# Four-token attention: relative scores by TensorE from folded weights, four of eight projections in front of the norm's last transposes, softmax in two halves

## The reference

```python
qkv = jnp.einsum('tbe,fe->tbf', query, in_proj_weight) + in_proj_bias
q, k, v = jnp.split(qkv, 3, axis=-1)
q = q * scaling                      # 8 ** -0.5
q, k, v = (heads(q), heads(k), heads(v))       # (b*16, t, 8)
dist = jnp.clip(r[None, :] - r[:, None], -L, L) + L
rel_k = rel_pos_keys[dist][:, :, :D]
scores = jnp.einsum('btd,bsd->bts', q, k) + jnp.einsum('btd,tsd->bts', q, rel_k)
probs = jax.nn.softmax(scores, axis=-1)
attn = jnp.einsum('bts,bsd->btd', probs, v)
return jnp.einsum('tbe,oe->tbo', attn, out_w) + out_b
...
x = _layernorm(x + _L2_attn_ref(x, ...), axis=-1)
```

## Time and profile before

| | before |
|---|---|
| median of three runs | 1515.82 us (1515.19 to 1516.74) |
| the profiled execution | 1518.54 us |
| its span | 1516.8 us |
| PE, DVE, ACT, POOL busy | 86%, 61%, 45%, 26% |
| mean granted clock of TensorE | 0.95 of 2.4 GHz |
| chain that ended last | PE 68%, DVE 18%, ACT 6%, issue 4%, POOL 4% |

### The profile page before, as it was taken

The page is one execution under the profiler, slowest core; times in us unless marked ns, Lnnn a source line. Parts: engine busy times, 40 slices in busy tenths (PEclk is TensorE's granted clock), DMA queues, the critical chain, the costliest instruction groups (busy, mean ns, idle before and its releaser), DMA issues.

```text
span 1516.8 us, 23793 instructions
## 1 busy us (share of the span) xinstructions
PE 1308.2 (86%) x8985; PEld 834.7 (55%) x8985; DVE 928.5 (61%) x2179; ACT 676.6 (45%) x1915; POOL 398.8 (26%) x326
## 2 busy tenths in 40 slices
PE   7999986888787878868987379899898999999997
PEld 4666663565555533325564345556565666666664
DVE  2555577666664689986755777555674555653343
ACT  4555444465664465524642035523345555432322
POOL 1333104443432177736100252010001333400000
PEclk9999999999999998979998699999999999999999
DMA  9000000000000054410002200000000000000000
GB/s 392 20 1 1 1 1 1 1 1 1 1 1 2 26 149 124 123 48 1 2 1 112 112 1 2 1 1 1 1 3 1 1 1 1 1 1 1 0 7 8
DMA packets 13280, 43.75 MB, mean 29 GB/s; under 512 B 1776, under 2 KB 3952, under 8 KB 12528
## 3 DMA queue, kind: packets, MB, share of 16 engines
q1 hardware_dynamic: 13168, 42.24, 8.2%
HBM read 41.58 MB, written 0.66 MB: 28 GB/s over the span
## 4 chain that ended last, share of the span: by engine, by line
PE 68%; DVE 18%; ACT 6%; issue 4%; POOL 4%; DMA 1%; DVEq 0%; SPq 0%; POOLq 0%; ACTq 0%
PE PS L1147 6%; PE PS L692 6%; PE PS L1097 4%; PE PS L1098 4%; PE PS L335 4%; DVE PS L2237 4%; PE PS L367 4%; PE PS L347 3%; PE PS L758 3%; PE PS L308 2%; PE PS L316 2%; PE PS L376 2%; PE PS L329 2%; PE PS L310 2%; DVE arena L2244 2%
## 5 line engine op out<-in xcount | busy, mean ns | idle before, releaser
L559 POOL TENSOR_TENSOR arena<-arena,small 128x768 f32<-128x768 f32 (+1 forms) x64 | 107.8, 1684 | 226.6 <-DVE small L502 117.7
L916 DVE TENSOR_REDUCE arena<-PS 128x2 f32<-128x512 f32 (+1 forms) x192 | 108.8, 609 | 54.9 <-PE PS L686 53.9
L850 ACT ACTIVATE arena<-PS 128x512 f32<-128x512 f32 (+1 forms) x192 | 92.2, 532 | 106.4 <-PE PS L692 106.4
L1243 DVE TENSOR_TENSOR arena<-arena,PS 128x512 f32<-128x512 f32 x82 | 56.3, 687 | 109.9 <-ACT arena L1107 109.8
L1107 ACT ACTIVATE arena<-PS 128x512 f32<-128x512 f32 x82 | 49.0, 598 | 162.0 <-PE PS L1098 162.0
L2044 PE MATMUL PS<-arena,w_consts 128*128 128x512 f32 x128 | 86.1, 761 | 34.1 <-DVE arena L2244 32.0
L439 ACT ACTIVATE arena<-PS,small 128x256 f32<-128x256 f32 (+1 forms) x256 | 110.8, 453 | 0.0
L692 PE MATMUL PS<-arena 32*128 32x256 f32 (+1 forms) x768 | 96.8, 368 | 14.0 <-DVE arena L916 9.0
L686 PE MATMUL PS<-arena 32*128 32x256 f32 (+1 forms) x768 | 93.8, 369 | 2.3 <-DVE arena L916 1.6
L510 DVE COPY arena<-PS 128x768 f32<-128x768 f32 (+1 forms) x64 | 69.5, 1086 | 34.5 <-PE PS L347 34.5
L2288 POOL TENSOR_TENSOR arena<-arena 128x512 f32<-128x512 f32 x64 | 80.4, 1270 | 36.4 <-DVE PS L2237 27.1
(11 more groups left out here) (408 smaller groups left out, 3021.4 us busy)
## 6 DMA issues: line engine op xcount, KB each, us to landing
arena<-rows SPq DMA_DIRECT2D x32, 512.0 KB, 4.8
w_last<-in_last SPq DMA_DIRECT2D x1, 8260.0 KB, 22.3
w_rest<-in_rest SPq DMA_DIRECT2D x1, 6463.5 KB, 38.1
w_last<-in_first SPq DMA_DIRECT2D x1, 4917.5 KB, 22.1
w_last<-in_first SPq DMA_DIRECT2D x1, 2176.0 KB, 10.2
w_last<-in_mid SPq DMA_DIRECT2D x1, 768.0 KB, 4.2
X<-in_x SPq DMA_DIRECT2D x1, 512.0 KB, 4.3
CT<-in_ctxT SPq DMA_DIRECT2D x1, 512.0 KB, 10.9
```

What stands on the lines that cost most here:

```text
L559: g.tensor_tensor(p, p, ri, ALU.mult).then_inc(self.pn_done.sem, 1)
L850: a.activation(self.PT[:, q % 8, :], PS[:, 3 + q % 3, 0:2 * n], ACT.Exp).then_inc(self.e_done.sem, 1)
L916: v.tensor_reduce(dst, src, AX.X, ALU.max, negate=True).then_inc(self.mx_done.sem, 1)
```

## The change

The relative part of the scores is linear in x: q times the relative keys is x times (query weights times relative keys), plus the query bias times the relative keys. One matmul folds the weights (`wqt` with `rel`, a block matrix of the relative keys by head), ScalarE copies the product into `fold`, and eight matmuls of 64 columns a tile give all relative scores in bank 6, on top of a matmul that writes the bias part. VectorE multiplies queries and keys straight from QKV and adds bank 6 afterwards; POOL has nothing to do. The scale moves into Exp. L2a becomes the norm's lead: the fold and projections 0 to 3 stand in front of the transposes of tiles 6 and 7, in place of five warming passes; the four warming passes behind the transposes are gone. Maxima, subtraction, Exp, sums, reciprocal and normalisation work on tiles 0 to 3 and 4 to 7 apart, the first half's maxima while products are still to come. Values times probabilities is one instruction a tile, not four; the subtraction and the normalisation one a half. Seven warming passes wait for the second subtraction. The output bias is written into banks 6 and 7 by a matmul with one row of ones, ahead of the output projection, which adds to it.

```diff
             self.transposes(pe, len(self.groups) - 1)
-            if not isinstance(self.lead, Experts):
+            if not isinstance(self.lead, (Experts, FourTokenAttention)):
                 keep_warm(self.c, pe, 3, 4)
...
+    def project(self, pe, n):
+        c = self.c
+        if n >= 4:
+            pe.wait_ge(self.p_ev.sem, self.p_ev.at(0, n - 3))
+        pe.matmul(c.PS[:, 2 + n % 4, 0:384], c.XT[:, n * P:(n + 1) * P], self.win, start=True, stop=True)\
+            .then_inc(self.p_done.sem, 1)
+    def lead_tensor(self, pe):
+        c = self.c
+        c.wait_weights(pe, self)
+        pe.matmul(c.PS[:, 7, 0:256], self.wqt, self.rel, start=True, stop=True).then_inc(self.fold_done.sem, 1)
+        pe.wait_ge(self.x_ready.sem, self.x_ready.at(0, 1 if self.led else 2))
+        for n in range(4):
+            self.project(pe, n)
+    def lead_scalar(self, a):
+        self.c.wait_weights(a, self)
+        a.wait_ge(self.fold_done.sem, self.fold_done.at(0, 1))
+        a.activation(self.fold, self.c.PS[:, 7, 0:256], ACT.Copy).then_inc(self.fold_ev.sem, 1)
     def tensor(self, pe):
         c, PS = self.c, self.c.PS
+        if not self.led:
+            self.lead_tensor(pe)
+        pe.matmul(PS[:, 6, :].rearrange("p (t u k) -> p t u k", t=4, u=2), self.bq.to_broadcast([P, P]),
+                  self.rel.rearrange("p (t k) -> p t k", t=4).unsqueeze(2).to_broadcast([P, 4, 2, 64]),
+                  start=True, stop=False, skip_group_check=True)
         pe.wait_ge(self.x_ready.sem, self.x_ready.at(0, 2))
+        for n in range(4, T):
+            self.project(pe, n)
+        pe.wait_ge(self.fold_ev.sem, self.fold_ev.at(0, 1))
         for n in range(T):
-            if n >= 4:
-                pe.wait_ge(self.p_ev.sem, self.p_ev.at(0, n - 3))
-            pe.matmul(PS[:, 2 + n % 4, 0:384], c.XT[:, n * P:(n + 1) * P], self.win, start=True, stop=True)\
-                .then_inc(self.p_done.sem, 1)
+            ins = pe.matmul(PS[:, 6, n * 64:n * 64 + 64], c.XT[:, n * P:(n + 1) * P],
+                            self.fold[:, n // 2 * 64:n // 2 * 64 + 64], start=False, stop=n == T - 1, skip_group_check=True)
+        ins.then_inc(self.rel_done.sem, 1)
+        pe.wait_ge(self.sh_ready.sem, self.sh_ready.at(0, 2))
+        keep_warm(c, pe, 7, 7)
         for n in range(T):
             pe.wait_ge(self.pv_ready.sem, self.pv_ready.at(0, n + 1))
-
             for k in range(4):
                 ins = pe.matmul(PS[:, n // 4, (n % 4) * P:(n % 4) * P + P], self.PV[:, n % 4, k * P:(k + 1) * P],
                                 c.ident, start=(k == 0), stop=(k == 3), skip_group_check=True)
-            if n < 3:
-                ins.then_inc(self.pv_used.sem, 1)
+            ins.then_inc(self.pv_used.sem, 1)
             if n % 4 == 3:
-                ins.then_inc(self.at_done.sem, 1)
+                pe.matmul(PS[:, 6 + n // 4, :].rearrange("p (t f) -> p t f", t=4), c.one[0:1, :].to_broadcast([1, P]),
+                          self.bout[0:1, :].unsqueeze(1).to_broadcast([1, 4, P]), start=True, stop=False,
+                          skip_group_check=True).then_inc(self.at_done.sem, 1)
         for n in range(T):
             if n % 4 == 0:
                 pe.wait_ge(self.at_ev.sem, self.at_ev.at(0, n // 4 + 1))
             ins = pe.matmul(PS[:, 6 + n // 4, (n % 4) * P:(n % 4) * P + P], self.AT[:, n * P:(n + 1) * P], self.wout,
-                            start=True, stop=True)
+                            start=False, stop=True, skip_group_check=True)
             if n % 4 == 3:
                 ins.then_inc(self.y_done.sem, 1)
     def scalar(self, a):
         c, PS = self.c, self.c.PS
-        a.wait_ge(self.sh_ready.sem, self.sh_ready.at(0, 1))
-        a.activation(self.sc, self.sc, ACT.Exp).then_inc(self.e_ready.sem, 1)
+        if not self.led:
+            self.lead_scalar(a)
+        for i in range(2):
+            a.wait_ge(self.sh_ready.sem, self.sh_ready.at(0, i + 1))
+            sc = self.sc[:, 4 * i:4 * i + 4, :]
+            a.activation(sc, sc, ACT.Exp, scale=8.0 ** -0.5).then_inc(self.e_ready.sem, 1)
         for i in range(2):
             a.wait_ge(self.at_done.sem, self.at_done.at(0, i + 1))
             a.activation(self.AT[:, i * 512:(i + 1) * 512], PS[:, i, :], ACT.Copy).then_inc(self.at_ev.sem, 1)
     def gpsimd(self, g):
...
+        pass
...
         v.wait_ge(self.p_ev.sem, self.p_ev.at(0, T))
...
+        def products(n):
+            pd = self.PD[:, n % 2, :]
+            v.tensor_tensor(pd.rearrange("p (s f) -> p s f", s=4), self.QKV[:, n % 2:T:2, 128:256],
+                            self.QKV[:, n, 0:128].unsqueeze(1).to_broadcast([P, 4, P]), ALU.mult).then_inc(self.prod.sem, 1)
+        def sums(n):
+            v.wait_ge(self.prod.sem, self.prod.at(0, n + 1))
+            return v.tensor_reduce(self.sc[:, n, :], self.PD[:, n % 2, :].rearrange("p (g d) -> p g d", d=8), AX.X, ALU.add)
+        def half(i):
+            r = slice(4 * i, 4 * i + 4)
+            sc, mx = self.sc[:, r, :], self.mx[:, r, :]
+            return (sc, mx, sc.rearrange("p n (s h) -> p n h s", s=4), sc.rearrange("p n (s h) -> p n s h", s=4),
+                    mx.unsqueeze(2).to_broadcast([P, 4, 4, 16]))
+        products(0)
         for n in range(T):
...
+            if n + 1 < T:
+                if n >= 1:
+                    link(sums(n - 1))
+                products(n + 1)
+            if n == T - 1:
+                sums(n - 1)
+                link(sums(n))
+            if n in (5, T - 1):
+                i = n // 6
+                sc, mx, by_head, by_key, spread = half(i)
+                if i == 0:
+                    v.wait_ge(self.rel_done.sem, self.rel_done.at(0, 1))
+                link(v.tensor_tensor(sc, sc, PS[:, 6, i * 256:i * 256 + 256].rearrange("p (n k) -> p n k", n=4), ALU.add))
+                link(v.tensor_reduce(mx, by_head, AX.X, ALU.max))
+                v.tensor_tensor(by_key, by_key, spread, ALU.subtract).then_inc(self.sh_ready.sem, 1)
+        for i in range(2):
+            sc, mx, by_head, by_key, spread = half(i)
+            v.wait_ge(self.e_ready.sem, self.e_ready.at(0, i + 1))
+            link(v.tensor_reduce(mx, by_head, AX.X, ALU.add))
+            link(v.reciprocal(mx, mx))
+            link(v.tensor_tensor(by_key, by_key, spread, ALU.mult))
+            for n in range(4 * i, 4 * i + 4):
+                if n >= 4:
                     v.wait_ge(self.pv_used.sem, self.pv_used.at(0, n - 3))
...
+                val = self.QKV[:, n % 2:T:2, 256:384].rearrange("p s (h d) -> p s h d", d=8)
+                p = by_key[:, n % 4].unsqueeze(3).to_broadcast([P, 4, 16, 8])
+                v.tensor_tensor(self.PV[:, n % 4, :].rearrange("p (s h d) -> p s h d", s=4, h=16), val, p, ALU.mult)\
+                    .then_inc(self.pv_ready.sem, 1)
         for i in range(2):
             v.wait_ge(self.y_done.sem, self.y_done.at(0, i + 1))
-            z = c.Z[:, 4 * i:4 * i + 4, :]
-            y = PS[:, 6 + i, :].rearrange("p (t f) -> p t f", t=4)
-            link(v.tensor_tensor(z, y, c.X[:, 4 * i:4 * i + 4, :], ALU.add))
-            ins = v.tensor_tensor(z, z, self.bout.unsqueeze(1).to_broadcast([P, 4, P]), ALU.add)
+            ins = v.tensor_tensor(c.Z[:, 4 * i:4 * i + 4, :], PS[:, 6 + i, :].rearrange("p (t f) -> p t f", t=4),
+                                  c.X[:, 4 * i:4 * i + 4, :], ALU.add)
         ins.then_inc(self.z_ready.sem, 1)
...
     rel = w["L2_attn_rel_pos_keys"][13:20, 0:8]
+    by_head = np.zeros((16, 8, 4, 4, 16), np.float32)
+    for h in range(16):
+        by_head[h, :, :, :, h] = np.stack([rel[3 - t:7 - t].T for t in range(4)], 1)
     l2a = [("L2a_win", w["L2_attn_in_proj_weight"].T), ("L2a_bin", over(w["L2_attn_in_proj_bias"])),
-           ("L2a_rel", np.broadcast_to(np.tile(rel, (1, 16)), (P, 7, P))), ("L2a_wout", w["L2_attn_out_w"].T),
+           ("L2a_wqt", w["L2_attn_in_proj_weight"][0:P]), ("L2a_bq", w["L2_attn_in_proj_bias"][0:P, None]),
+           ("L2a_rel", by_head.reshape(P, 256)), ("L2a_fold", np.zeros((P, 256), np.float32)), ("L2a_wout", w["L2_attn_out_w"].T),
            ("L2a_bout", over(w["L2_attn_out_b"]))]
...
-            if isinstance(s, (TwoWay, Experts)) or isinstance(s, NarrowAttention) and s.band is None:
+            if isinstance(s, (TwoWay, Experts, FourTokenAttention)) or isinstance(s, NarrowAttention) and s.band is None:
                 end.lead, s.led = s, True
```

More of the change, by code:

```diff
@@ L1799, with __init__ @@
 class FourTokenAttention:
-    def __init__(self, c, win, bin_, relk, wout, bout):
-        self.c, self.win, self.bin, self.relk, self.wout, self.bout = c, win, bin_, relk, wout, bout
-        self.x_ready = c.x_ready
+    def __init__(self, c, win, bin_, wqt, bq, rel, fold, wout, bout):
+        self.c, self.win, self.bin, self.wout, self.bout = c, win, bin_, wout, bout
+        self.wqt, self.bq, self.rel, self.fold = wqt, bq, rel, fold
+        self.x_ready, self.led = c.x_ready, False
         s = c.sig
```

(40 more changed lines are left out.)

1 line of the change is left out of this document (removed).

## The result

The changed kernel takes 1503.53 us (median of four runs, 1499.76 to 1507.62) against 1515.51 us (1510.94 to 1516.74): ratio 0.9918, 95% interval 0.9898 to 0.9938. The forecast was 1504.0 us in 1500.8 to 1507.8. A second set of five runs on another occasion gave 0.9931 (0.9919 to 0.9944), so the gain is some 10 to 12 us. The profiled execution took 1507.62 us with a span of 1505.8, which is 11.0 us less than the span before.

A forecast was written before the change was run, and what follows sets the result against it. Stage L2a was taken as one serial string of about 46.5 us across engines. Gains 3.9 + 1.9 + 3.6 - 0.9 + 3.2, say 11.8 us, off 1515.8 gave 1504.0 us, range 1500.8 to 1507.8.

The forecast's parts named there:

- In front of the stage: Norm before L2a: fold and projections 0 to 3 fill TensorE's idle time; evictions end at 830.6, not 834.48, gaining 3.9 us.
- the first rival: TensorE's clock falls near 826.6 as before, slowing projections 4 to 7: 2.9 us lost, 1506.9 us; chance 0.2.
- The scale and POOL's additions: Step from the last eviction at 834.48 to the first product at 836.41 goes, scale rides in Exp: gain 1.9 us.
- products: VectorE's eight query-key products take 0.68 us each with POOL at rest, bounds 0.68 and 1.14.
- the second rival: Products take 1.14 us even with POOL at rest, reading keys in place being slow: 3.7 us lost, 1507.7; chance 0.05.
- The size of the pairs: VectorE's eight product-and-sum pairs take 1.44 us each, 11.5 in all, against 1.89 each before: gain 3.6 us.
- From t to the end: From the second subtraction's end (t) to the stage's end: 15.4 us instead of 18.6, gain 3.2 us.
- The halves: Relative-score addition, maxima and subtraction on VectorE in two halves: 3.1 us against 2.2 before, loss 0.9 us.
- The third rival: The high clock outlives the stage, speeding the next norm's warming passes and first matmuls: 1.3 to 1.5 us more, 1502.5; chance 0.15.
- The fourth: Rival: the low clock is held on in the stage behind, L2x, making the program slower than before: 1518 us; chance 0.03.
- fifth: Rival: the change does not do what it says, relative scores or lead coming too late: about 1507 us; chance 0.02.
- that drift: Part of the forecast's spread: about 1 us where clock edges fall in later stages.

The follow-up runs named there:

- r2: Changed kernel without the lead, five and four warming passes back: 1506.77 us, ratio to before 0.9948; L190 to last addition 40.1 us against 34.0.
- r9: Kernel before with POOL's additions left out, keys read from QKV: 1507.05 us, one run; L190 to last addition 41.2 us against 47.2.
- r5: Changed kernel with eight unused POOL additions of 128x512 beside the products: 1509.66 us, one run; L190 to last addition 37.3 us against 34.0.
- r10: Changed kernel with the second output-bias matmul in TensorE's idle time behind the relative scores, seven warming passes kept: 1500.16 us, ratio to before 0.9895.
- r12: Changed kernel with softmax in one piece, second output-bias matmul in idle time, and TensorE warming through the products: 1502.61 us, one run.
- r6: Changed kernel with eight warming passes behind the first subtraction and five behind the second: 1500.46 us, ratio to before 0.9892.
- r4: Changed kernel with the second output-bias matmul ahead of PV and three warming passes instead of seven: 1501.37 us, ratio to before 0.9916.
- r8: Changed kernel with the softmax in one piece instead of halves: 1505.97 us, one run; L190 to last addition 36.9 us against 34.0.
- r7: Changed kernel with warming behind the first subtraction too, and one warming pass, then the second output-bias matmul, before PV: 1503.08 us, ratio 0.9917.

## Why the prediction was right

**In front of the stage: right, and the first rival fell.** The evictions took 4.5 us from the norm's last tile, where 4.8 was forecast; the bias matmul and projections 4 to 7 ran at the high level. In the three profiles without the lead (before, r2, r9) the clock fell 1.4 to 1.5 us behind the start of L190; in the eleven with it, it did not fall within 8 us. So the lead, with what it replaces, holds the clock up. The first rival's price, 2.9 us for a fallen clock with the lead in place, was never met: r2 loses 5.5 us, but only 1.7 of them to the clock.

**The scale and POOL's additions, products: right.** 1.9 us gained, and then 0.69 a product. r5 puts POOL back and gets the slow product, r9 takes it from the kernel before and gets the fast one: the second rival, reading in place, is out on both sides.

**The size of the pairs was off by 1 us.** I took 1.44 a pair from the kernel before, whose product waited for POOL and whose sum waited for the product of the same tile. With products one tile ahead, an instruction starts up to 0.08 us before the end that the trace gives the one in front: 1.32 a pair. From the first product to t: 13.35 us against 14.6 in the forecast. The half reduce (0.580), the addition (0.417) and the reciprocal (0.553) came out as worked out, where the formula of the Trainium skill (VectorE: DVE Perf Modes, on the trn2 errata), taken for the reduces too, gives 0.42 and not 0.58.

**From t to the end: 15.5 us against 15.4, by errors that cancel.** The clock rose 3.3 us behind the first warming pass, not 4.7, which saves 0.7. Against it, each bias matmul takes 1.05 us in the chain and not 0.87, 0.4 for the two; and a tile of PV takes 0.94 us at the high level (3.77 for four) and not 0.88, some 0.4 more for eight. That the second bias matmul is on the path was forecast, and r10 bears it out with 1.1 us. The halves, which cost 0.9 us ahead of t in my sum, pay behind it: r12 puts them at a net gain of 1.5 us.

**The third rival came half true.** The clock outlived the stage and fell at 864.5, 0.9 us into the next norm's transposes, too early for the warming passes behind them; L2x gained nothing and even lost 1.2 us, with a second episode of low clock that no rival had. The fourth and fifth did not occur.

**The sum.** 13.2 us in the stretch against 11.8 forecast: 4.2 us for the evictions (3.9 forecast), 1.9 up to the first product (1.9), 4.0 from there to t (2.7) and 3.1 behind t (3.2). No run prices alone what the merged instructions (values, subtraction, normalisation) give. That the program's median still lies 0.5 us from the forecast is luck to that extent: in the profiled execution some 2 us were given back outside the stretch (1.7 behind it, 0.4 in front), and runs of one kernel differ by some 8 us. I had put that drift at about 1 us, which is the mis-sized part of the range. Whether the give-back is systematic stays open; across the profiles the time behind the stretch lies between 641.9 and 649.6 us with the same code.

## What to carry to other kernels

Fill TensorE's waits in front of a stage with that stage's own independent matmuls: they are out of the queue when it gets long, which was the larger part here, and they hold the clock for what follows. When POOL and VectorE share a serial loop, ask what POOL's help costs VectorE's two-input instructions before counting the work it takes off. Put a small matmul that initialises a bank where its engine idles, not in front of the signal that others wait for, and judge such edits on the stretch that they touch, since a program's time also moves with clock edges in stages they don't.

## What the runs showed of the hardware

- A matmul of one row costs TensorE no less than one of 128 rows: 1.12 us for the two passes of 512 columns of L1874, 1.04 for those of L1853, both at the high level (1.05 and 0.87 in the chain).
- The same code of L3a took 82.4 us at a mean granted clock of 0.98 and 86.2 at 0.92. The first part of L2f took 63.7 at 0.95 and 60.9 at 1.00.
- A warming train does not bring the clock up at a fixed distance. Counted from the subtraction that releases it (the first pass of a train is missing from some traces): 3.4 us in the changed kernel, 4.0 in r6, 4.7 in r2, 6.9 in r4, 8.7 in r8, 12.4 in r7.
- A POOL addition beside them costs VectorE's two-input products of 128x512 0.4 us each (0.691 to 1.086) and its one-input sums nothing (0.678 and 0.673).
